# Turned copies of the input: laid out by the host and fetched, in place of two transposes and an eviction in each tile

## Chip, core and metric

The kernel runs on one NeuronCore of a Trainium2 chip. Its engines are TensorE (PE: matrix products; PEld is its weight load), VectorE (DVE), ScalarE (ACT), GpSimd (POOL) and SyncE (SP), which here only issues transfers. Each runs its own list of instructions in order and waits on semaphores for the others. The metric is the time of one execution on the device in microseconds, median of the runs.

## The reference

The input x is 8 x 750 x 256 in fp32. The calculation is one layer of three parts, each added to its input:

```python
# token mixing: segments of 256 tokens, every second token kept (128 rows per segment)
scores = einsum('bsqd,bskd->bsqk', x, x) / sqrt(256)
h = softmax(scores) @ x
# holographic attention, on layernorm(h)
bound = circ_conv(n, bind_key)                  # n = layernorm(h)
hologram = decay_matrix @ bound                 # causal, d ** (t - s)
h = h + n + gate * circ_corr(hologram, unbind_key)
# mixture of experts, on xf = layernorm(h), v = 0, two iterations:
#   shared control and 8 experts, of which 2 are chosen by a router, 512 -> 64 -> 768, gelu
#   integrator: sigmoid, softplus and a halting gate update (x, v)
# refining: 256 -> 512 -> 256 with gelu, times integration_weight
h = h + xf + integration_weight * refined
```

For a score product x . x^T of a 128-row tile TensorE needs x with its 256 features along the partitions, in two pieces of 128: the turned tile, xT.

## The kernel before

There are 24 tiles of 128 rows (8 batches of 3 segments; the third has 119 rows and is filled with zeros). The work is a software pipeline written out by hand: the function `slot(t)` of each engine is run for t = -3 to 26, and in one slot seven tiles are at work. z = t+3 is turned and its scores are computed; e = t+2 goes through exp; f = t+1 through attention, both layernorms, the scan, the router; t through the first expert iteration; n = t-1 through the second; m = t-2 through the integrator's end; o = t-3 through refining and output. What follows in which order on an engine is just the order of the code; waits are written by `passed(engine, semaphore, tile)`. A slot here is counted from TensorE's refining layer, ctl<-x2T (slot 3 is the first that has one).

For tile z in a slot, before the change: SP fetched the plain tile into one of six buffers xa (L299). TensorE turned it with two transposes into the PSUM bank pc (L623), after the scan of tile f had read that bank. ScalarE evicted it to the single buffer xT (L897, 128x256), between exp of tile e (L891) and the softplus of tiles m and t, for which another table of functions is loaded (L776). TensorE, after the 32 pieces of the experts' hidden layer (L427, pa<-x1T), multiplied xT with itself (L644) into pd, and VectorE scaled the scores and took their minimum (L1166, two records). Then xf of tile f was turned into pc (L652), which waited until xT had left that bank, and evicted by ScalarE (L793), after the table of the gelus (L787). Of xfT TensorE makes the router's hidden layer (L427, cd<-xfT; waits for xfT and for the scaled scores, which share the bank pd).

Ahead of the slots SP fetches the weights, all in one queue: the first plain tile, ident, the parameters `keeping(1)` (465 KB, from which ScalarE and VectorE make their constants), and so on. In the first slot that has a tile f (t = -1) ScalarE casts weights (`constants()`, L754 to L760), after the eviction of tile 2, and VectorE makes their low parts (`low_parts()`, L1023 and L1027), after xf of tile 0 and before the scaling of tile 2's scores. GpSimd computes u = xf - mu (L390) and base (L355, L357) from the same xf.

## Time and profile before

| | |
|---|---|
| median of 3 runs | 816.12 us (815.87 to 817.86) |
| the profiled execution | 814.5 us, of which the span from first to last instruction is 812.6 |
| TensorE products | 749.5 us busy, 92% of the span |
| TensorE weight loads | 650.0 us, 80% |
| VectorE | 651.9 us, 80% |
| ScalarE | 536.0 us, 66% |
| GpSimd | 274.1 us, 34% |
| chain that ended last | PE 46%, DVE 24%, ACT 21%, issue 8%, DMA 1% |
| mean granted TensorE clock | 0.966 of full speed |
| transfers | 14.13 MB in all; the 16 engines are 8 tenths busy in the first 20 us, 1 tenth in the next, near 0 after |

A profile is one execution. Engines overlap, so busy shares say which are full, not what bounds; the chain of waits says which piece of work, on which engine, every later piece was waiting for. A timeline row is start, duration, engine, line, operation, output and inputs, shapes; in brackets the idle time before it and what ended it. The granted clock is 1.00 at 2.4 GHz and 0.50 at 1.2 GHz.

### The profile page before, as it was taken

What the parts mean: (1) busy time and instruction counts of PE and PEld (TensorE: products, weight loads), DVE (VectorE), ACT (ScalarE), POOL (GpSimd) and SP (SyncE); (2) the same over time, 40 slices, a digit from 0 to 9 for tenths busy, and PEclk for the clock granted to TensorE, in tenths of its full rate; (3) what the DMA queues carried; (4) which work ended last, traced back from release to release, by engine and by line L of the source; (5) the groups of instructions that cost most, each with busy time, mean ns of one, the idle gap of its engine ahead of it and who ended that gap; (6) DMA issues with size and microseconds to landing.
All of it is one profiled execution on the core that took longest, in us unless ns stands there. A gap on an engine that the chain in (4) does not pass through costs nothing.

```text
span 812.6 us, 14659 instructions
## 1 busy us (share of the span) xinstructions
PE 749.5 (92%) x4784; PEld 650.0 (80%) x4784; DVE 651.9 (80%) x1516; ACT 536.0 (66%) x1334; POOL 274.1 (34%) x393
## 2 busy tenths in 40 slices
PE   4578999999999999999999999999999999999884
PEld 3466888888888888888888888888888888888764
DVE  3447778888889889889889889889889889889652
ACT  1555667677676676676676676685685785775554
POOL 1134333243253252243243243234234334333121
PEclk9577999999999999999999999999999999999997
DMA  8100000000000000000000000000000000000000
GB/s 336 52 8 1 1 1 14 1 15 14 1 14 11 5 14 7 8 15 1 15 13 2 14 14 1 14 14 1 14 14 2 8 8 1 8 8 1 7 8 13
DMA packets 8154, 14.13 MB, mean 17 GB/s; under 512 B 848, under 2 KB 7048, under 8 KB 7568
## 3 DMA queue, kind: packets, MB, share of 16 engines
q1 hardware_dynamic: 8080, 13.20, 4.6%
q8 instruction: 39, 0.64, 0.3%
q14 instruction: 35, 0.29, 0.1%
HBM read 10.05 MB, written 3.15 MB: 16 GB/s over the span
## 4 chain that ended last, share of the span: by engine, by line
PE 46%; DVE 24%; ACT 21%; issue 8%; DMA 1%; POOL 0%; ACTq 0%; POOLq 0%; SPq 0%; DVEq 0%
PE ctl L450 9%; PE ctl L466 7%; PE ctl L427 5%; ACT L776 3%; DVE hm_hi L1040 3%; PE pb L427 3%; ACT ge L809 3%; ACT L787 3%; PE ctl L469 2%; PE pa L427 2%; ACT work L779 2%; DVE both L1208 2%; ACT work L783 2%; PE cd L615 2%; DVE gl L1054 2%
## 5 line engine op out<-in xcount | busy, mean ns | idle before, releaser
L347 POOL TENSOR_TENSOR hm_lo<-gl,mexp 128x256 fp32r<-128x256 f32 x144 | 111.2, 797 | 358.5 <-DVE gl L1054 358.5
L450 PE MATMUL ctl<-w2e_hi,hm_hi 128*128 128x512 f32 (+1 forms) x432 | 160.6, 381 | 10.3 <-DVE hm_hi L1040 10.1
L450 PE MATMUL ctl<-w2e_lo,hm_hi 128*128 128x512 f32 (+1 forms) x432 | 149.6, 360 | 0.0
L827 ACT ACTIVATE work<-ctl 128x256 f32<-128x256 f32 (+1 forms) x144 | 70.6, 490 | 90.3 <-PE ctl L469 90.3
L450 PEld LDWEIGHTS ctl<-w2e_hi,hm_hi 128*128 128x128 f32 x432 | 82.1, 190 | 28.0 <-DVE hm_hi L1040 16.4
L466 PE MATMUL ctl<-w2e_hi,hm_lo 128*128 128x512 f32 (+1 forms) x432 | 102.3, 362 | 0.1
L1040 DVE TENSOR_TENSOR hm_hi<-ge,mexp 128x256 fp32r<-128x256 f32 x144 | 79.4, 579 | 22.3 <-ACT ge L809 16.1
L450 PEld LDWEIGHTS ctl<-w2e_lo,hm_hi 128*128 128x128 f32 x432 | 82.5, 191 | 11.1
L427 PE MATMUL pa<-x1T,par 128*128 128x128 f32 x768 | 89.7, 275 | 0.0
L427 PEld LDWEIGHTS pa<-x1T,par 128*128 128x128 f32 x768 | 87.8, 192 | 0.1
L466 PEld LDWEIGHTS ctl<-w2e_hi,hm_lo 128*128 128x128 f32 x432 | 74.3, 188 | 14.7 <-POOL hm_lo L347 0.8
L809 ACT ACTIVATE ge<-pa,par 128x128 f32<-128x128 f32 x192 | 54.6, 371 | 13.1 <-PE pa L427 13.1
L427 PE MATMUL pa<-xfT,par 128*128 128x128 f32 x384 | 55.8, 291 | 0.0
L829 ACT ACTIVATE work<-ctl 128x256 f32<-128x256 f32 x144 | 55.0, 382 | 0.0
L427 PEld LDWEIGHTS ctl<-x2T,par 128*128 128x128 f32 x384 | 47.9, 197 | 4.3 <-issue 1.3
L427 PEld LDWEIGHTS pa<-xfT,par 128*128 128x128 f32 x384 | 50.1, 203 | 1.1
L427 PE MATMUL ctl<-x2T,par 128*128 128x128 f32 x384 | 48.7, 282 | 1.5 <-issue 1.0
L456 PE MATMUL ctl<-w2a,hm_hi 128*128 128x512 f32 (+1 forms) x144 | 47.8, 386 | 0.0
L800 ACT ACTIVATE sh<-pb,par 128x128 f32<-128x128 f32 x48 | 17.6, 367 | 44.4 <-PE pb L427 44.4
L1070 DVE TENSOR_SCALAR work<-work,w 128x256 f32<-128x256 f32 x72 | 43.3, 655 | 2.9 <-ACT work L829 2.8
L469 PE MATMUL ctl<-w2b,end 128*128 128x512 f32 (+2 forms) x144 | 43.8, 358 | 1.3 <-ACT end L822 1.3
L949 ACT ACTIVATE end<-cd 116x256 fp32r<-116x256 f32 x24 | 9.2, 384 | 52.6 <-PE cd L721 52.6
(167 smaller groups left out, 1733.7 us busy)
## 6 DMA issues: line engine op xcount, KB each, us to landing
work<-params_dram SPq DMA_DIRECT2D x3, 1152.0 KB, 10.3
out_dram<-y SPq DMA_DIRECT2D x24, 128.0 KB, 1.7
xa<-x_dram SPq DMA_DIRECT2D x16, 128.0 KB, 2.7
par<-params_dram SPq DMA_DIRECT2D x1, 1280.0 KB, 12.8
work<-params_dram SPq DMA_DIRECT2D x2, 512.0 KB, 11.1
xa<-x_dram SPq DMA_DIRECT2D x8, 119.0 KB
par<-params_dram SPq DMA_DIRECT2D x1, 512.0 KB, 15.9
par<-params_dram SPq DMA_DIRECT2D x1, 465.0 KB, 4.6
```

The source lines that it names most:

```text
L347: TT(hm[1][:, j, c, :], gl[:, c, :], pairs(tile, j, c), ALU.mult).then_inc(done, 1)
L427: last = mm(dst[0:rows, c * P:(c + 1) * P], w[:, q, c, :], rhs[:, q, :], start=(q == 0), stop=(q == nk - 1))
L450: mm(dst[:, a:z], hm[0][:, j, c, :], w2e[i][:, c, a:z], start=(c == 0 and i == 0), stop=False)
L456: mm(dst[:, a:z], hm[0][:, j, PC, :], w2a[:, 1 + j, a:z], start=False, stop=False)
L466: mm(dst[:, a:z], hm[1][:, j, c, :], w2e[0][:, c, a:z], start=False, stop=False)
L469: last = mm(dst[:, a:z], end[tile.s][0:rows, j, :], w2b[0:rows, 1 + j, a:z], start=False, stop=True)
L776: nc.scalar.preload_act_table_set("softplus")
L809: last = AF(ge[:, c, :], pa[:, c * P:(c + 1) * P], ACT.Gelu, bias=par[:, a:a + 1])
L827: AF(tan[tile.s][:, 1:kinds, j, :], ctl_t[:, D:kinds * D].rearrange("p (a d) -> p a d", a=kinds - 1), ACT.Tanh, scale=0.5)
L829: AF(rb[tile.s][:, j, :], ctl_t[:, 0:D], ACT.Copy).then_inc(done, 1)
L1040: V.tensor_tensor(hm[0][:, j, c, :], ge[:, c, :], pairs(tile, j, c), ALU.mult).then_inc(done, 1)
L1070: last = V.tensor_scalar(gw[:, j, :], tan[m.s][:, 1, j, :], 1.0, w3[m.s][:, j:j + 1], ALU.add, ALU.mult)
```

## The change

The host lays the input out a second time: for each tile the kept rows, turned, 128 partitions x 256 (`_turned`). SP fetches that into three buffers xT, one for each segment of a batch; the first three are issued among the first transfers, the others each right behind the plain tile. The transposes, the eviction and their two semaphores are gone. The score product waits for the transfer, the attention product (L559) for the plain tile's transfer, which the transposes had waited for, and the transposes of xf for the scan of their tile, as the removed ones did.

```diff
@@ -103,7 +103,7 @@
 ENDS = [slice(0, HID), slice(HID, P)]
 
 
-def audio_layer(nc, x, params, out):
+def audio_layer(nc, x, turned_x, params, out):
     fp32, f32r, bf16 = mybir.dt.float32, mybir.dt.float32r, mybir.dt.bfloat16
     u32 = mybir.dt.uint32
     ALU, ACT, AX = mybir.AluOpType, mybir.ActivationFunctionType, mybir.AxisListType
@@ -172,7 +172,7 @@
 
 
         xa = [sb(f"xa{s}", [P, D]) for s in range(NX)]
-        xT = sb("xT", [P, KD, P])
+        xT = [sb(f"xT{s}", [P, KD, P]) for s in range(NS)]
         sc = sb("sc", [P, P])
         nmx = sb("nmx", [P, NS])
         ex = sb("ex", [P, P])
@@ -244,20 +244,21 @@
...
         x_in = [sem(f"x_in{s}") for s in range(NX)]
+        xT_in = [sem(f"xT_in{s}") for s in range(NS)]
...
@@ -298,14 +299,21 @@
                 src = x_pairs[bass.ds(tile.b * (SEQ // DIL) + tile.s * P, rows), 0:D]
                 sp.dma_start(xa[tile.x][0:rows, :], src).then_inc(x_in[tile.x], 16)
 
+            def turned_in(tile):
+                sp.dma_start(xT[tile.s][:, :, :].rearrange("p k m -> p (k m)"),
+                             turned_x[bass.ds(tile.n * P, P), :]).then_inc(xT_in[tile.s], 16)
+
             x_pairs = x.rearrange("(r two) d -> r (two d)", two=DIL)
+            turned_in(Tile(0, 0))
+            keeping(0)
             tile_in(Tile(0, 0))
-            keeping(0)
+            turned_in(Tile(0, 1))
             keeping(1)
             tile_in(Tile(0, 1))
             staging(0)
             sp.wait_ge(pad_zero, 1)
             tile_in(Tile(0, 2))
+            turned_in(Tile(0, 2))
             staging(1, E)
             staging(2)
             staging(5)
@@ -319,6 +327,8 @@
                 if z.exists() and z.low > 2:
                     passed(sp, att_ps, z, back=NX)
                     tile_in(z)
+                    passed(sp, score_ps, z, back=NS)
+                    turned_in(z)
                 if o.exists():
                     passed(sp, y_v, o)
                     sp.dma_start(out[bass.ds(o.n * P, P), :], y[o.s][:, :]).then_inc(y_out[o.s], 16)
@@ -536,8 +546,6 @@
                     passed(pe, ex_sb, f)
                     if t.exists():
                         passed(pe, me_sb, t, per=2, step=1)
-                    else:
-                        passed(pe, xT_sb, f)
                     nc.tensor.transpose(pc[:, 0:P], ex[:, :], ident).then_inc(eT_ps, 1)
                     if f.low == 0:
                         bound_and_back()
@@ -556,6 +564,7 @@
                         passed(pe, me_sb, t, per=2)
                     else:
                         passed(pe, smax_v, f.at(1))
+                    pe.wait_ge(x_in[f.x], 16 * (f.turn + 1))
                     mm(pd[:, 0:D], eT[:, :], xa[f.x][:, :], start=True, stop=True).then_inc(att_ps, 1)
 
                 if n.exists():
@@ -615,14 +624,6 @@
                         last = mm(pd[:, 0:D], holo[f.s][:, q, :], mix[:, q, :], start=(q == 0), stop=(q == KD - 1))
                     last.then_inc(retr_ps, 1)
 
-                if z.exists():
-                    pe.wait_ge(x_in[z.x], 16 * (z.turn + 1))
-                    if f.exists():
-                        passed(pe, scan_v, f)
-                    for q in range(KD):
-                        last = nc.tensor.transpose(pc[:, q * P:(q + 1) * P], xa[z.x][:, q * P:(q + 1) * P], ident)
-                    last.then_inc(xT_ps, 1)
-
                 if n.exists():
                     if t.exists():
                         passed(pe, e1_sb, t, per=2)
@@ -635,19 +636,18 @@
                     refine_lo(o)
 
                 if z.exists():
-                    passed(pe, xT_sb, z)
+                    pe.wait_ge(xT_in[z.s], 16 * (z.b + 1))
                     if f.exists():
                         passed(pe, mv2_v, f)
                     else:
                         passed(pe, smax_v, z, back=1)
                     for q in range(KD):
-                        last = mm(pd[:, 0:P], xT[:, q, :], xT[:, q, :], start=(q == 0), stop=(q == KD - 1))
+                        last = mm(pd[:, 0:P], xT[z.s][:, q, :], xT[z.s][:, q, :], start=(q == 0), stop=(q == KD - 1))
                     last.then_inc(score_ps, 1)
 
                 if f.exists():
                     passed(pe, xf_v, f)
-                    if z.exists():
-                        passed(pe, xT_sb, z)
+                    passed(pe, scan_v, f)
                     for q in range(KD):
                         last = nc.tensor.transpose(pc[:, q * P:(q + 1) * P], xf[f.s][:, q * P:(q + 1) * P], ident)
                     last.then_inc(xfT_ps, 1)
@@ -890,11 +890,6 @@
                     passed(act, eT_ps, e, back=1)
                     AF(ex[:, :], sc[:, :], ACT.Exp, scale=-1.0, bias=nmx[:, e.s:e.s + 1],
                        accum_out=esum[:, e.s:e.s + 1]).then_inc(ex_sb, 1)
-
-                if z.exists():
-                    passed(act, xT_ps, z)
-                    passed(act, score_ps, z, back=1)
-                    AF(xT[:, :, :].rearrange("p k m -> p (k m)"), pc[:, 0:D], ACT.Copy).then_inc(xT_sb, 1)
 
                 if t.exists():
                     softplus_of(m, t)
@@ -1293,6 +1288,15 @@
     return np.concatenate([a[n] for n, _ in _ALL], axis=1)
 
 
+def _turned(x):
+
+    import numpy as np
+    rows = np.zeros((BATCH, NS * P, D), np.float32)
+    rows[:, 0:SEQ // DIL] = x[:, ::DIL]
+    tiles = rows.reshape(NT, P, KD, P).transpose(0, 3, 2, 1)
+    return np.ascontiguousarray(tiles).reshape(NT * P, KD * P)
+
+
 def kernel(**inputs):
     import numpy as _np
     import concourse.bacc as _bacc
@@ -1300,7 +1304,8 @@
     from concourse.bass_utils import run_bass_kernel_spmd as _run
 
     i = {k: _np.asarray(v) for k, v in inputs.items()}
-    arrays = {"x_dram": _np.ascontiguousarray(i["x"].reshape(BATCH * SEQ, D)), "params_dram": _pack(i)}
+    arrays = {"x_dram": _np.ascontiguousarray(i["x"].reshape(BATCH * SEQ, D)), "turned_dram": _turned(i["x"]),
+              "params_dram": _pack(i)}
     nc = _bacc.Bacc("TRN2", target_bir_lowering=False, num_devices=1)
     args = [nc.dram_tensor(n, a.shape, _mybir.dt.from_np(a.dtype), kind="ExternalInput").ap()
             for n, a in arrays.items()]
```

On ScalarE, in a slot of the steady part, before:

```order
L891 ACTIVATE ex,esum<-sc,nmx 128x128
L897 ACTIVATE xT<-cd 128x256
L776 ACT_TABLE_LOAD
L779 ACTIVATE work<-work 128x768
L783 ACTIVATE work<-work 128x3x256
L787 ACT_TABLE_LOAD
L793 ACTIVATE xfT<-cd 128x256
```

and changed (exp, table, two softplus, table, eviction of xf):

```order
L891 ACTIVATE ex,esum<-sc,nmx 128x128
L776 ACT_TABLE_LOAD
L779 ACTIVATE work<-work 128x768
L783 ACTIVATE work<-work 128x3x256
L787 ACT_TABLE_LOAD
L793 ACTIVATE xfT<-cd 128x256
```

One row is gone, and nothing else moved. On ScalarE at the start, before (small holds constants, w2b and w2e_hi are casts of weights):

```order
L749 ACTIVATE small<-par 128x1
L750 ACTIVATE small<-par 128x1
L897 ACTIVATE xT<-cd 128x256
L891 ACTIVATE ex,esum<-sc,nmx 128x128
L897 ACTIVATE xT<-cd 128x256
L847 ACTIVATE eT<-cd 128x128
L891 ACTIVATE ex,esum<-sc,nmx 128x128
L897 ACTIVATE xT<-cd 128x256
L787 ACT_TABLE_LOAD
L754 ACTIVATE identb<-par 128x128
L756 ACTIVATE expandb<-work 8x512
L758 ACTIVATE w2b<-work 128x2304
```

and changed:

```order
L749 ACTIVATE small<-par 128x1
L750 ACTIVATE small<-par 128x1
L891 ACTIVATE ex,esum<-sc,nmx 128x128
L847 ACTIVATE eT<-cd 128x128
L891 ACTIVATE ex,esum<-sc,nmx 128x128
L787 ACT_TABLE_LOAD
L754 ACTIVATE identb<-par 128x128
L756 ACTIVATE expandb<-work 8x512
L758 ACTIVATE w2b<-work 128x2304
```

The table load and the casts now follow exp of tile 1 directly. On SP's queue, the first transfers before:

```order
L299 DMA xa<-x_dram 128x256
L288 DMA par<-params_dram 128x128
L288 DMA par<-params_dram 128x930
L299 DMA xa<-x_dram 128x256
L288 DMA work<-params_dram 128x1024
```

and changed:

```order
L303 DMA xT<-turned_dram 128x256
L289 DMA par<-params_dram 128x128
L300 DMA xa<-x_dram 128x256
L303 DMA xT<-turned_dram 128x256
L289 DMA par<-params_dram 128x930
L300 DMA xa<-x_dram 128x256
L289 DMA work<-params_dram 128x1024
```

The parameters for the constants (128x930) stand behind two more transfers.

## Rows read from the trace of the kernel before

**Rows 1.** Busy time by stretches of the trace; columns in the first line.
```profile
core 0: us, PE busy (x) PEld busy (x) DVE busy (x) ACT busy (x) POOL busy (x), PEclk, DMA share, GB/s
60.00:91.00 31.00, 26.95 (x150) 22.25 (x148) 21.58 (x49) 18.79 (x47) 13.10 (x17) 0.81 0.00 1
...
312.30:343.20 30.90, 30.17 (x201) 26.44 (x201) 26.92 (x63) 21.64 (x57) 11.13 (x16) 1.00 0.03 9
...
682.90:713.20 30.30, 29.43 (x194) 25.71 (x193) 26.45 (x60) 21.15 (x55) 11.78 (x16) 1.00 0.02 6
```

**Rows 2.** The chain of waits: start, length, what. Starts of slots 3, 21, 22.
```profile
127.07 1.79 PE ctl L427 x16
...
682.87 1.79 PE ctl L427 x16
...
713.25 1.79 PE ctl L427 x16
```

**Rows 3.** The chain of waits inside slot 8.
```profile
293.20 0.01 ACT xT L897
...
293.59 1.28 ACT L776
...
309.11 0.44 PE cd L736 x2
```

**Rows 4.** Timeline of ScalarE: slot 9 (two rows) and slot 21.
```profile
323.79 0.19 ACT L891 ACTIVATION_READ_ACCUMULATOR ex<-sc,nmx 128x1 f32 x1
...
324.50 1.28 ACT L776 ACT_TABLE_LOAD   x1
...
694.56 1.28 ACT L776 ACT_TABLE_LOAD   x1
```

**Rows 5.** Timeline of VectorE and GpSimd: slot 8, then slot 21.
```profile
295.76 1.38 DVE L1080 TENSOR_TENSOR work<-work 128x768 f32<-128x768 f32 x1 [0.24 <-ACT work L779]
297.18 0.69 DVE L1081 TENSOR_TENSOR both<-work 128x512 f32<-128x512 f32 x1
...
298.12 0.08 DVE L1166 DVE_READ_ACCUMULATOR sc<-cd 128x1 f32 x1
...
696.91 0.95 DVE L1080 TENSOR_TENSOR work<-work 128x768 f32<-128x768 f32 x1
697.89 1.10 DVE L1081 TENSOR_TENSOR both<-work 128x512 f32<-128x512 f32 x1
...
697.07 1.38 POOL L390 TENSOR_TENSOR u<-xf,par 128x256 f32<-128x256 f32 x1 [0.53 <-DVE xf L1153]
```

**Rows 6.** Timeline of TensorE: slot 8.
```profile
298.35 0.62 PE L427 MATMUL cd<-xfT,par 128*64 128x128 f32 x4
299.28 0.50 PE L450 MATMUL ctl<-w2e_hi,hm_hi 128*128 128x512 f32 x1 [0.31 <-DVE hm_hi L1040]
```

**Rows 7.** Timeline of the first 40 us: SP's queue, TensorE, ScalarE, VectorE, GpSimd.
```profile
2.11 0.43 SPq L299 DMA_DIRECT2D xa<-x_dram  x1
...
10.51 1.22 PE L644 MATMUL cd<-xT 128*128 128x128 f32 x4 [1.97 <-ACT xT L897]
...
21.84 0.38 ACT L897 ACTIVATE xT<-cd 128x256 f32<-128x256 f32 x1 [9.20 <-PE cd L623]
...
26.41 2.88 DVE L1023 SCALAR_TENSOR_TENSOR w2b<-w2b,par,work 128x768 fp32r<-128x768 f32 x3 [2.54 <-ACT w2b L758]
...
25.43 0.72 POOL L357 TENSOR_TENSOR base<-base,ib 128x256 f32<-128x256 f32 x1
...
32.07 1.08 PE L427 MATMUL cd<-xfT,par 128*64 128x128 f32 x4 [7.46 <-issue]
```

**Rows 8.** The chain of waits at the start and in slot 1.
```profile
1.65 4.61 DMA par<-params_dram
...
9.36 0.31 DVE sc L1166 x2
...
79.98 0.27 ACT xT L897
```

More of the change, by code:

```diff
@@ L250, in audio_layer @@
         dve_link = sem("dve_link")
-        (xT_ps, score_ps, eT_ps, att_ps, xnT_ps, retr_ps, xfT_ps, rh_ps, lg_ps, mT_ps, me_ps, s1_ps, e1_ps,
+        (score_ps, eT_ps, att_ps, xnT_ps, retr_ps, xfT_ps, rh_ps, lg_ps, mT_ps, me_ps, s1_ps, e1_ps,
          halt1_ps, u1_ps, x1T_ps, s2_ps, e2_ps, halt2_ps, u2_ps, x2T_ps, rl1_ps, rl2_ps) = (
-            sem(n) for n in ("xT_ps score_ps eT_ps att_ps xnT_ps retr_ps xfT_ps rh_ps lg_ps mT_ps me_ps s1_ps "
+            sem(n) for n in ("score_ps eT_ps att_ps xnT_ps retr_ps xfT_ps rh_ps lg_ps mT_ps me_ps s1_ps "
                              "e1_ps halt1_ps u1_ps x1T_ps s2_ps e2_ps halt2_ps u2_ps x2T_ps rl1_ps rl2_ps").split())
-        (xT_sb, ex_sb, eT_sb, xfT_sb, rh_sb, tw_sb, mT_sb, me_sb, s1_sb, e1_sb, th1_sb, u1_sb, x1T_sb, s2_sb,
+        (ex_sb, eT_sb, xfT_sb, rh_sb, tw_sb, mT_sb, me_sb, s1_sb, e1_sb, th1_sb, u1_sb, x1T_sb, s2_sb,
          e2_sb, th2_sb, u2_sb, x2T_sb, rg_sb, sp1_sb, sp2_sb, gh1_sb, gh2_sb,
          rgh_sb, eb1_sb, eb2_sb) = (
-            sem(n) for n in ("xT_sb ex_sb eT_sb xfT_sb rh_sb tw_sb mT_sb me_sb s1_sb e1_sb th1_sb u1_sb x1T_sb "
+            sem(n) for n in ("ex_sb eT_sb xfT_sb rh_sb tw_sb mT_sb me_sb s1_sb e1_sb th1_sb u1_sb x1T_sb "
                              "s2_sb e2_sb th2_sb u2_sb x2T_sb rg_sb sp1_sb sp2_sb gh1_sb gh2_sb rgh_sb eb1_sb eb2_sb").split())
```

## Prediction

> **What bounds the kernel now.** I read the busy time by stretches first [rows 1]. In a slot of the steady part TensorE is busy 30.17 of 30.90 us; so a stage is worth anything only where it can be heard through a nearly full TensorE. Then the whole chain of waits, for the length of a slot: the 16 pieces of the refining layer begin at 127.07 in slot 3 and at 682.87 in slot 21, 18 slots, 30.88 us each [rows 2]. Then the chain inside one slot [rows 3]. It has three legs: TensorE from the transposes of x2 (309.11) through the next slot's products up to the hidden layer of the shared expert; then ScalarE for about 9.5 us (two gelus, a table load, exp, **the eviction into xT**, a table load, two softplus, a table load, the eviction into xfT, four gelus, the split copy); then VectorE up to x2. TensorE stands still in the last two legs only for moments: 0.31 us before the expert product, which waits for the masked units [rows 6]. So ScalarE's leg decides, and the eviction that goes is a link of it: the table load of L776 starts at 293.59, where exp's read-out was over and the eviction could begin at 293.20.
>
> **What goes, per slot.** (a) The eviction on ScalarE. In one slot of three, as that of rows 3, 293.59 - 293.20 = 0.39 us. In the two others it also waited for its transposes: read-out of exp ends at 323.79 + 0.19 = 323.98, table load at 324.50 [rows 4]; without it the load follows after 0.02, so 0.50. Over 18 slots 12 x 0.50 + 6 x 0.39 = 8.3. (b) Two transposes on TensorE, 0.22 us from start to start; they lie ahead of a stall, so they are no gain of their own, but TensorE has to come earlier too if ScalarE's 0.50 is to be passed on: 0.22 and the 0.31 of the stall cover it. (c) Transposes of xf no longer wait for the eviction; they came long after it: nothing.
>
> **The slot that is already without it.** Slot 21 has no tile to prepare: no transposes, no eviction, no score product, no scaling of scores. From 682.87 to 713.25 it takes 30.38 us [rows 2], 0.50 less than the mean, with TensorE at 29.43 of 30.30 busy and the granted clock at 1.00 [rows 1]; its table load starts at 694.56 [rows 4], 0.20 after exp's read-out began. 18 x 0.50 = 9.0. It also lacks the score product and VectorE's scaling, which stay in the changed kernel, so it is the upper end; I take 8.5 for the 18 slots.
>
> **What is late next in a slot.** The first product of the router waits for xfT and for VectorE's scaling of the scores. The scaling's read-out ends at 298.12 + 0.08 = 298.20 and that product starts at 298.35 [rows 5, 6]: they stand 0.15 apart, so the scaling must come earlier as well. Ahead of it VectorE does L1080 and L1081. Before, L1080 waited 0.24 us for a softplus, started at 295.76 and took 1.38, because GpSimd was in its own operation on xf; in slot 21, where the softplus came earlier, it started at 696.91, ahead of GpSimd (697.07, which then took 1.38 in place of 0.73), and took 0.95, and L1081 took 1.10 in place of 0.69 [rows 5]. From the moment at which VectorE was free for L1080 to the end of L1081 that is 297.18 + 0.69 - (295.76 - 0.24) = 2.35 before and 697.89 + 1.10 - 696.91 = 2.08 in slot 21. So the scaling comes about 0.3 earlier, and so does the router's product; 0.1 to 0.2 that it lacks to ScalarE's 0.50 is slack, since ScalarE gets to that product's gelu only after the four gelus of the experts.
>
> **The first slots.** In slot 1 the piece of the eviction that shows in the chain is 0.27 [rows 8]; slot 2 has the same piece, slot 0 I estimate at 0.4 like a steady one. Together 0.9.
>
> **The start** is where the change is largest and least sure. ScalarE stood 9.20 us until the third tile's transposes, evicted at 21.84, and only then loaded its table and cast the weights; VectorE waited 2.54 us for the first cast, until 26.41, with xf ready at 23.87 [rows 7]. From 26.41 to the router's first product at 32.07 the work is a fixed string of 5.66 us. Changed, ScalarE goes on to the casts from 21.84 - 9.20 = 12.64 on, as the weights land, and has 11 us for a table load and two casts; VectorE then starts when xf is there: 2.54 gained at most. Against it, three things. First, two more transfers are issued ahead of the parameters that feed ScalarE's and VectorE's constants; an issue takes 0.43 [rows 7], so those land 0.86 late at least, and if the 256 KB also move ahead of the 465 KB that took 4.61 from issue to landing [rows 8], up to 256/465 x 4.61 = 2.5 more. I take 1.2, near the lower end, since the two transfers move while the later ones are issued. Second, in favour: the score product of tile 1 stood at 10.51 for its eviction [rows 7], though the scaling of tile 0 was over at 9.36 + 0.31 = 9.67 [rows 8]; this gives 0.8 back. Net delay of the string 0.4. Third, VectorE now meets GpSimd: three operations of GpSimd on xf and h2, of 0.72 each, the last at 25.43 [rows 7], were finished before VectorE began at 26.41; now they fall on it. One such meeting cost VectorE 0.41 (1.10 against 0.69, rows 5), three make 1.2. Start: 2.54 - 0.4 - 1.2 = 0.9, bounded by 2.54 (no delay) and by 2.54 - 2.6 - 2.2, a loss of 2.3.
>
> That the one waits for the other is what rows 5 show on both sides; how much of the other it waits for is open between 0.41 and the whole 0.72 (rival 3). The Trainium skill (SBUF — State Buffer, section "SBUF: two separate sides") says that a VectorE operation with two inputs in SBUF and a GpSimd operation that reads SBUF take a shared port pair in turns, whichever comes second waiting for the whole of the other. By that the sum is the one of rival 3, by rows 5 the one below; slot 21's VectorE waited for less than the rule has it.
>
> **Nothing for the transfers in the slots.** A turned tile is issued right behind its plain tile, a slot and more ahead of its use, and the transfer engines are at 0.03 of their time there [rows 1]. SP's new wait (score of the tile three before) is for a product two slots old, so the output behind it in the queue is not held. TensorE's new wait for the plain tile in the attention product is for a transfer of slots ago.
>
> **Sum.** 8.5 + 0.9 + 0.9 = 10.3. The profiled execution of before took 814.5 us (span 812.6 and 1.9 around it), so 804.2; the median of the runs, 816.12, lies 1.6 above that execution, and I forecast the median: 805.8 us.
>
> **Rivals.**
> 1. VectorE's scaling doesn't move (GpSimd gets ahead of L1080 as before). The router's product stays at 298.35, its gelu can come only 0.2 earlier, and a slot gains 0.2 to 0.25 although ScalarE is free sooner: 18 x 0.22 = 4.0, with the 0.9 of the start and the 0.9 of the first slots 5.8 gained, 810.3. Against it: slot 21 did it the other way. 0.10.
> 2. TensorE's clock in the first slots. From 60 to 91 the granted clock is 0.81 on average [rows 1], that is 38% of 31 us at 1.2 GHz, after a stretch in which TensorE stood still for parts of slot 0. With 0.4 us less standing still there the clock may stay at 2.4 GHz: up to 0.19 x 31 = 5.9 less, 799.9. For it: nothing else stands ahead of that stretch. Against it: most of the standing still remains. 0.07.
> 3. At the start VectorE waits for the whole of each GpSimd operation: 3 x 0.72 = 2.2 in place of 1.2; the start gives 2.54 - 0.4 - 2.2 = 0, the sum is 9.4, the time 806.7. It differs from the forecast by less than the runs do, but its trace is another one: the string of 5.66 us takes 7.9. 0.15.
> 4. The gain is swallowed within measuring (another engine's string just as late everywhere), 815 to 817: slot 21 speaks against it. 0.02.
> 5. Slower: TensorE's clock falls in the steady part, because it now has less work in a slot. Price: a slot of 30.17 us of TensorE at half speed, some 25 to 30 us more, so 830; a microsecond at 1.2 GHz costs half of one, so it decides once more than 2 x 10.3 = 21 us of the steady part are run so. Slot 21, with still less work than a changed slot will have, kept 1.00. 0.03, with whatever else could make it slower by as much.
>
> **How the numbers follow.** The forecast has 0.63. Its own width: the start from a loss of 2.3 to a gain of 2.5, the slots from 7.3 (18 x 0.39 and a little more) to 9.0, 0.5 us of run to run; 803.5 to 809. The range takes in part of rival 2 and stops short of rival 1's centre: 802.8 to 809.6. A change under 0.3% (2.4 us) can't be told from none here; rivals 4 and 5 alone lie there or beyond: faster 0.95, same 0.02, slower 0.03.
>
> **What would show it.** Right: slots of 30.4 us throughout, all three kinds alike; L776 0.02 behind exp's read-out; L1080 near 0.95 us and GpSimd's operation on xf stretched to 1.4; the casts on ScalarE before 24, VectorE's low parts right behind xf but with three GpSimd operations between them, the string at 6.9 us in place of 5.66; the router's first product near 31.2. Wrong: L1080 still at 1.38 and slots near 30.65 (rival 1); a stretch of the granted clock that differs between 44 and 91; the parameters landing later than 7.5 us; or a new wait ahead of the score product.

## The result, and the profile after

| | before | changed |
|---|---|---|
| median of the runs | 816.00 us | 806.23 us |
| lowest, highest, runs | 813.73, 817.86, 4 | 804.91, 806.45, 4 |
| profiled execution, its span | 814.5, 812.6 us | 804.9, 803.1 us |
| granted clock, whole span | 0.966 | 0.968 |

The ratio is 0.9878, with a 95% interval from 0.9851 to 0.9905: 9.8 us faster. The forecast was 805.8 us (802.8 to 809.6). The transfers grow from 14.13 to 17.28 MB; the host's work of laying the input out a second time is not in the metric.

In the changed kernel the lines of its own file moved: L427 is now L437 (hidden and refining products), L450 is L460 (experts), L592 is L601, L615 is L624, L644 is L645, L541 is L549, and on VectorE L1080 is L1075, L1081 is L1076, L1166 is L1161, L1114 is L1109, L1128 is L1123, L1023 is L1018; on GpSimd L390 is L400. ScalarE's lines up to L891 kept their numbers.

**The length of a slot.** The chain of waits of the changed kernel: start, length, what. Slots 3, 4, then 8, 9, 10, then 21 and 22.
```profile
125.25 1.79 PE ctl L437 x16
155.68 1.79 PE ctl L437 x16
...
277.43 1.78 PE ctl L437 x16
307.87 1.79 PE ctl L437 x16
338.33 1.79 PE ctl L437 x16
...
673.24 1.79 PE ctl L437 x16
703.67 1.79 PE ctl L437 x16
```
From 125.25 to 673.24 are 18 slots: 30.44 us each, where [rows 2] gave 30.88. That is 18 x 0.44, or 682.87 - 127.07 - (673.24 - 125.25) = 7.81 us. The kinds are nearly alike now: 30.43 for slot 3, 30.44 for slot 8, 30.46 for slot 9. Up to slot 3 the changed kernel leads by 127.07 - 125.25 = 1.82, and from slot 21 on it loses 0.13, since 803.1 - 673.24 is 129.86 and 812.6 - 682.87 is 129.73. Together 9.5, the difference of the two spans.

**ScalarE's leg in slot 8.** Timeline of ScalarE: start, length, engine, line, operation.
```profile
288.96 0.19 ACT L891 ACTIVATION_READ_ACCUMULATOR ex<-sc,nmx 128x1 f32 x1
289.17 1.28 ACT L776 ACT_TABLE_LOAD   x1
...
293.36 0.39 ACT L793 ACTIVATE xfT<-cd 128x256 f32<-128x256 f32 x1
```
The table load stands 0.02 behind the end of exp's read-out, 0.21 behind its start. In [rows 3] the eviction stood between them, in [rows 4] the eviction and its wait.

**VectorE, GpSimd and TensorE in slot 8**, from their timelines; in square brackets the idle time before, and what ended it.
```profile
291.39 0.95 DVE L1075 TENSOR_TENSOR work<-work 128x768 f32<-128x768 f32 x1
292.38 1.10 DVE L1076 TENSOR_TENSOR both<-work 128x512 f32<-128x512 f32 x1
...
293.73 0.08 DVE L1161 DVE_READ_ACCUMULATOR sc<-cd 128x1 f32 x1
```
```profile
291.56 1.38 POOL L400 TENSOR_TENSOR u<-xf,par 128x256 f32<-128x256 f32 x1 [0.53 <-DVE xf L1148]
```
```profile
293.96 0.62 PE L437 MATMUL cd<-xfT,par 128*64 128x128 f32 x4
294.87 0.49 PE L460 MATMUL ctl<-w2e_hi,hm_hi 128*128 128x512 f32 x1 [0.29 <-DVE hm_hi L1035]
```
This is slot 21 of [rows 5] to the hundredth: 0.95, 1.10, and 1.38 on GpSimd, with VectorE ahead. The expert product still stands for the masked units, 0.29 in place of the 0.31 of [rows 6].

**Stretches**, the same columns as in [rows 1]: us, busy time of TensorE, its weight loads, VectorE, ScalarE, GpSimd, then clock, transfers, GB/s.
```profile
60.00:91.00 31.00, 27.18 (x141) 22.17 (x142) 20.40 (x48) 18.16 (x44) 13.10 (x17) 0.81 0.02 5
307.90:338.30 30.40, 29.93 (x199) 26.21 (x199) 26.81 (x63) 21.24 (x56) 11.79 (x16) 1.00 0.05 14
```
TensorE is busy 29.93 of 30.40 us, and the granted clock stays 1.00: the two transposes are gone, and the slot shrank by more than they had filled.

**The start.** Timelines of ScalarE, VectorE, GpSimd and TensorE in the first 33 us.
```profile
7.39 0.20 ACT L749 ACTIVATE small<-par 128x1 f32<-128x1 f32 x1 [5.38 <-DMA par<-params_dram]
...
13.04 1.28 ACT L787 ACT_TABLE_LOAD   x1
...
17.09 2.11 ACT L760 ACTIVATE w2e_hi<-work 128x2304 fp32r<-128x2304 f32 x1
```
```profile
23.82 0.41 DVE L1148 TENSOR_SCALAR xf<-h,mv,rs 128x256 f32<-128x256 f32 x1 [0.94 <-POOL rs L396]
24.15 3.81 DVE L1018 SCALAR_TENSOR_TENSOR w2b<-w2b,par,work 128x768 fp32r<-128x768 f32 x3
27.88 3.07 DVE L1022 TENSOR_TENSOR w2e_lo<-work,w2e_hi 128x2304 fp32r<-128x2304 f32 x1
```
```profile
24.32 1.43 POOL L400 TENSOR_TENSOR u<-xf,par 128x256 f32<-128x256 f32 x1 [0.53 <-DVE xf L1148]
...
27.22 1.32 POOL L367 TENSOR_TENSOR base<-base,ib 128x256 f32<-128x256 f32 x1
```
```profile
31.26 1.09 PE L437 MATMUL cd<-xfT,par 128*64 128x128 f32 x4 [6.28 <-issue]
```
The casts stand from 13.04 on and are over at 19.20, far ahead of xf. VectorE no longer waits: it begins its low parts at 24.15, 2.26 earlier than the 26.41 of [rows 7]. But the three of them take 3.81 in place of 2.88, and GpSimd's three operations at the same time take 1.43, 1.43 and 1.32 in place of 0.72 each. From VectorE's start to the router's first product it is 31.26 - 24.15 = 7.11 us, where it was 5.66: of the 2.26 there remain 0.81.

### The profile page after: what moved, and what is told of

It reads as the page before. It is cut to its first block, busy times and chain, and to the rows that moved or that the text cites. A ratio compares the mean times of both kernels' runs of the same rounds, so it can differ in the third digit from the quotient of the medians.

```text
span 803.1 us, 14519 instructions
## 1 busy us (share of the span) xinstructions
PE 743.1 (93%) x4736; PEld 644.9 (80%) x4736; DVE 651.7 (81%) x1516; ACT 528.7 (66%) x1310; POOL 288.2 (36%) x393
## 2 busy tenths in 40 slices
DMA packets 11611, 17.28 MB, mean 22 GB/s; under 512 B 1232, under 2 KB 10504, under 8 KB 11024
## 4 chain that ended last, share of the span: by engine, by line
PE 42%; DVE 25%; ACT 24%; issue 8%; DMA 1%; POOL 0%; SPq 0%; POOLq 0%; ACTq 0%; DVEq 0%
PE ctl L460 9%; PE ctl L476 7%; PE ctl L437 5%; ACT L776 4%; ACT L888 4%; DVE hm_hi L1035 3%; ACT L787 3%; ACT ge L809 3%; PE pb L437 3%; PE ctl L479 2%; PE pa L437 2%; ACT work L779 2%; DVE both L1203 2%; ACT work L783 2%; DVE gl L1049 2%
## 5 line engine op out<-in xcount | busy, mean ns | idle before, releaser
L460 PE MATMUL ctl<-w2e_hi,hm_hi 128*128 128x512 f32 (+1 forms) x432 | 160.4, 381 | 8.6 <-DVE hm_hi L1035 8.2
L460 PE MATMUL ctl<-w2e_lo,hm_hi 128*128 128x512 f32 (+1 forms) x432 | 149.4, 360 | 0.0
L460 PEld LDWEIGHTS ctl<-w2e_hi,hm_hi 128*128 128x128 f32 x432 | 82.2, 190 | 26.2 <-DVE hm_hi L1035 14.6
L460 PEld LDWEIGHTS ctl<-w2e_lo,hm_hi 128*128 128x128 f32 x432 | 82.4, 191 | 11.1
L437 PEld LDWEIGHTS pa<-x1T,par 128*128 128x128 f32 x768 | 89.4, 192 | 1.1
L437 PE MATMUL pa<-x1T,par 128*128 128x128 f32 x768 | 89.6, 275 | 0.0
L437 PE MATMUL pa<-xfT,par 128*128 128x128 f32 x384 | 55.6, 291 | 0.0
L437 PEld LDWEIGHTS ctl<-x2T,par 128*128 128x128 f32 x384 | 47.8, 197 | 4.3 <-issue 1.3
L437 PEld LDWEIGHTS pa<-xfT,par 128*128 128x128 f32 x384 | 49.9, 202 | 1.1
L437 PE MATMUL ctl<-x2T,par 128*128 128x128 f32 x384 | 48.6, 281 | 1.5 <-issue 1.0
L381 POOL TENSOR_TENSOR rg_lo<-rg,rg_hi 128x512 fp32r<-128x512 f32 x24 | 31.1, 1297 | 35.5 <-ACT rg_hi L772 35.5
```

The source lines that it names most:

```text
L437: last = mm(dst[0:rows, c * P:(c + 1) * P], w[:, q, c, :], rhs[:, q, :], start=(q == 0), stop=(q == nk - 1))
L460: mm(dst[:, a:z], hm[0][:, j, c, :], w2e[i][:, c, a:z], start=(c == 0 and i == 0), stop=False)
```

## Experiments

Each is the changed kernel with an edit; those of e1, e2, e9 and e10 add work whose result nobody reads. Slot length is that of slots 3 to 20 from the chain of waits; the last column is the start of the router's first product.

| | median us | kernel before, same chip | ratio, 95% | slot us | router us |
|---|---|---|---|---|---|
| changed | 806.23 | 816.00 | 0.9878 (0.9851 to 0.9905) | 30.44 | 31.26 |
| e1 copy on ScalarE | 811.75 | 815.47 | 0.9966 (0.9948 to 0.9984) | 30.71 | 31.37 |
| e2 transposes back | 809.45 | 815.47 | 0.9924 (0.9896 to 0.9953) | 30.53 | 31.54 |
| e3 GpSimd first | 815.63 | 815.47 | 0.9995 (0.9979 to 1.0010) | 30.86 | 31.78 |
| e4 GpSimd late | 804.90 | 815.47 | 0.9881 (0.9856 to 0.9906) | 30.42 | 31.11 |
| e5 GpSimd off the start | 804.43 | 814.66 | 0.9870 (0.9839 to 0.9902) | 30.43 | 30.26 |
| e6 parameters first | 803.83 | 814.66 | 0.9864 (0.9835 to 0.9892) | 30.43 | 28.91 |
| e7 ScalarE held at the start | 805.85 | 814.66 | 0.9897 (0.9861 to 0.9933) | 30.43 | 32.94 |
| e8 = e4 + e5 + e6 | 802.45 | 814.66 | 0.9847 (0.9818 to 0.9875) | 30.43 | 27.94 |
| e9 slots as before, start as changed | 815.49 | 815.45 | 1.0002 (0.9987 to 1.0018) | 30.86 | 32.58 |
| e10 transposes and wait, no eviction | 807.81 | 815.45 | 0.9897 (0.9875 to 0.9920) | 30.52 | 31.27 |

**e1_copy.** A copy of a constant of the eviction's size, into a buffer that nobody reads, where the eviction stood.
```diff
+                if z.exists() and z.low > 2:
+                    AF(spare[:, :], pv("iw"), ACT.Copy)
                 if t.exists():
                     softplus_of(m, t)
```


> The changed kernel with one copy more on ScalarE (128x256, of a constant, into a buffer that nobody reads) where the eviction of xT stood, in the 21 slots from t = 0 on. Theory (ScalarE's leg sets the slot): the copy takes 0.36 to 0.38 us and all of it is heard, a slot goes from 30.44 to 30.8 us, 18 slots 6.7 us and the first three 1.1 more: 806.2 + 7.8 = 814.0 us. Rival (TensorE or VectorE set the slot of the changed kernel): 806 to 808.

The slot is 0.27 longer: (680.83 - 127.98) / 18 = 30.71. Timeline of ScalarE in this kernel, slot 8:
```profile
293.02 0.18 ACT L892 ACTIVATION_READ_ACCUMULATOR ex<-sc,nmx 128x1 f32 x1
293.12 0.40 ACT L896 ACTIVATE spare<-par 128x256 f32<-128x256 f32 x1
293.52 1.28 ACT L777 ACT_TABLE_LOAD   x1
```
The copy waits for nothing and so begins under the read-out, 0.10 behind its start; the table load stands 0.50 behind the read-out's start, against 0.21 without the copy, so ScalarE gave away 0.29, and the slot shows 0.27. ScalarE's leg is the one that decides, and what is laid on it is heard nearly whole; only the size of the piece was 0.3 and not 0.36.

VectorE in the same slot, its first product:
```profile
295.69 1.47 DVE L1078 TENSOR_TENSOR work<-work 128x768 f32<-128x768 f32 x1 [0.16 <-ACT work L780]
```
GpSimd had begun its operation on xf at 295.61, so it is ahead again, as in the kernel before; in slots 9 and 10 VectorE stays ahead (0.96). The slots take 30.73, 30.70 and 30.70 us all the same: while ScalarE is this late, the order costs nothing of its own.

**e2_turns.** The two transposes back on TensorE, with their waits; nobody reads what they make.
```diff
+                if z.exists():
+                    pe.wait_ge(x_in[z.x], 16 * (z.turn + 1))
+                    if f.exists():
+                        passed(pe, scan_v, f)
+                    for q in range(KD):
+                        nc.tensor.transpose(pc[:, q * P:(q + 1) * P], xa[z.x][:, q * P:(q + 1) * P], ident)
                 if n.exists():
...
                     hidden(pa, P, w1e, range(EC), x1T, 2 * KD, e2_ps)
```


> The changed kernel with the two transposes put back on TensorE at their old place in each of 24 tiles; nobody reads what they write. Theory (they lie ahead of a moment in which TensorE waits): the 0.22 us a slot go into the 0.29 us that the expert product waits; router's product 0.2 later, which leaves ScalarE's gelu 0.0 to 0.06 late; slot 30.44 to 30.5, time 806 to 807.5. Rival (TensorE's list is full): 0.22 x 21 = 4.6 more, 810.8.

30.53, so +0.09 and not nothing. It is not spread evenly; e10 below has where it goes.

**e3_u_first.** VectorE's products wait until GpSimd has made its operation on xf, so that the order of the kernel before is back, without the eviction.
```diff
                 if m.exists() and not last_in:
+                    if f.exists():
+                        passed(dve, u0_g, f)
                     products(m)
```


> The changed kernel in which VectorE's L1075 waits until GpSimd is through with u = xf - mu, so that GpSimd goes first and VectorE no longer overtakes it. This is rival 1 of the prediction made true. Theory: L1075 starts at about the end of u, 0.9 us later than now, both VectorE operations then run unhindered (0.95 and 0.69), the scaling ends 0.5 later than now, the router's product starts 0.5 later and ScalarE's gelu 0.3 later: slot near 30.75, 18 x 0.3 = 5.4 more, 811.6. Rival (slack there is larger than read): slot unchanged at 30.44, 806.2.

The whole gain is gone: 815.63 against 815.47, slots of (683.10 - 127.70) / 18 = 30.86. VectorE and TensorE in this kernel, slot 8:
```profile
296.92 0.96 DVE L1075 TENSOR_TENSOR work<-work 128x768 f32<-128x768 f32 x1 [0.84 <-POOL u L400]
```
```profile
299.08 0.62 PE L437 MATMUL cd<-xfT,par 128*64 128x128 f32 x4 [0.52 <-DVE sc L1163]
```
The router's product begins 299.08 - 282.04 = 17.04 us into its slot (the slot starts at 282.04), against 293.96 - 277.43 = 16.53 in the changed kernel: 0.51 later. ScalarE, at the gelu of what that product makes, now stands for it:
```profile
299.75 0.36 ACT L919 ACTIVATE rh<-cd,par 64x128 f32<-64x128 f32 x1 [0.23 <-PE cd L437]
```
The slot is 0.42 longer than the changed one on the mean, where I expected 0.3. So ScalarE's 0.4 can't be had in full unless VectorE's scaling of the scores comes earlier with it. How much is left without that, this run doesn't measure, since the edit puts the product later than the kernel before had it (17.04 against 298.35 - 281.52 = 16.83). An estimate: the gelu begins 17.71 into the slot here and began at 17.67 in the kernel before; with the product 0.21 earlier it would begin at 17.50, so about 0.2 a slot would be left, which is what rival 1 had.

**e4_u_late.** The reverse: GpSimd's operation on xf waits for the largest score, so it comes behind L1076.
```diff
                     passed(pool, x1_v, f, back=NS)
+                    if z.exists() and z.low > 2:
+                        passed(pool, smax_v, z)
                     TT(u0[f.s][:, :], xf[f.s][:, :], pv("mu"), ALU.subtract)
```


> The changed kernel in which GpSimd's u waits until VectorE has scaled the scores (tiles 3 to 23), so that L1076 isn't held up by it. Theory: L1076 takes 0.69 in place of 1.10 and the scaling comes 0.41 earlier, but the router's product is not what ScalarE waits for, so the slot stays 30.44 and the time 806.2. Rival (the scaling still sets when the router's product and with it the leg ends): slot 0.1 to 0.4 shorter, 799 to 804.

L1076 is back at 0.69 us and the scaling comes earlier, but VectorE then stands 0.98 before the masked units; slots 30.42. Once VectorE is ahead of GpSimd, more lead has no worth.

**e5_gpsimd_off_start.** GpSimd's first operation on xf waits until VectorE's low parts of the weights are done.
```diff
+                    if f.low == 0:
+                        pool.wait_ge(set_dve, 2)
                     TT(u0[f.s][:, :], xf[f.s][:, :], pv("mu"), ALU.subtract)
```


> The changed kernel in which GpSimd's three operations at the start (u and base of tile 0) wait until VectorE has made the low parts. Theory (VectorE pays for meeting GpSimd): the low parts go back from 3.81 + 3.07 us to 2.88 + 2.55, the router's first product from 31.26 to about 29.9, time 1.4 less, near 804.8, read with some 1 to 2 us of scatter from when TensorE's clock rises in the first 75 us. Rival (something else stretched them, as ScalarE's traffic or transfers): no change of either duration.

VectorE's timeline at the start of this kernel:
```profile
24.61 2.87 DVE L1020 SCALAR_TENSOR_TENSOR w2b<-w2b,par,work 128x768 fp32r<-128x768 f32 x3
27.39 2.55 DVE L1024 TENSOR_TENSOR w2e_lo<-work,w2e_hi 128x2304 fp32r<-128x2304 f32 x1
```
2.87 and 2.55 in place of 3.81 and 3.07, and the router's product 30.26 - 24.61 = 5.65 us behind VectorE's start, which is the string of before (5.66). So the 1.45 us by which the string had grown were the meetings with GpSimd. In the time of the kernel the 1.0 us is inside the scatter.

**e6_params_first.** The parameters are fetched ahead of the first two tiles and their turned forms.
```diff
+            keeping(1)
             turned_in(Tile(0, 0))
             keeping(0)
             tile_in(Tile(0, 0))
             turned_in(Tile(0, 1))
-            keeping(1)
```


> The changed kernel with the parameters for the constants (465 KB) first in SP's queue, ahead of the turned and plain tiles. Theory (the two transfers put ahead of them delayed the start by 1.1 us, from 6.28 to 7.39): ScalarE's first constant near 5.4, the router's first product 1.5 to 2 us earlier than 31.26 unless the weights for bind and unbind land later, time 804.2 to 804.8. Rival (the start is held by the big weights): the constants come earlier and the router's product stays within 0.3 of 31.26.

ScalarE's first constant, from its timeline in this kernel:
```profile
4.30 0.20 ACT L749 ACTIVATE small<-par 128x1 f32<-128x1 f32 x1 [2.29 <-DMA par<-params_dram]
```
4.30 in place of 7.39, and the router's first product at 28.91 in place of 31.26, 2.35 earlier, more than the 1.5 to 2 expected, as the constants too came earlier than the 5.4 expected. The time, 803.83, is below the changed kernel's, but the intervals of the two ratios overlap.

**e7_hold_scalar.** At the start ScalarE waits, before its table load and casts, as long as it did before the change, without the eviction.
```diff
+                if z.exists() and z.low == 2:
+                    passed(act, retr_ps, f)
                 if t.exists():
                     softplus_of(m, t)
```


> The changed kernel in which ScalarE waits, in the slot that casts weights, for the first retrieval product, as it waited for the third tile's transposes before the change; so the casts start at about 21.8 in place of 13.0. Theory: the first cast ends near 25.9, VectorE's low parts start there in place of 24.15, meet only the last GpSimd operation, and the router's first product is at 31.6 to 31.8 in place of 31.26: 0.4 later, 806.6. So of the start's gain the freed ScalarE is worth only 0.4, since GpSimd's meetings eat the rest. Rival (the early casts are worth the 2.5 us they are earlier): 808.7, router's product at 33.7.

VectorE waits again (1.70 for w2b) and starts at 26.90, when two of GpSimd's three operations are over; all three take 0.72 or 0.73, and only the last meets VectorE, whose product takes 3.26 there (2.87 without GpSimd in e5, 3.81 in the changed kernel). What that saves is less than the later start costs. From xf's start to the router's product it is 32.94 - 24.78 = 8.16, against 31.26 - 23.82 = 7.44: 0.72 lost, where I expected 0.4. In the time nothing of it can be seen (805.85).

**e9_slots_back.** Transposes, wait and eviction back, the eviction from t = 0 on and into a buffer that nobody reads; the transfers, and ScalarE's list at the start, stay as changed.
```diff
+                    if z.low > 2:
+                        passed(act, turn_ps, z)
+                        AF(spare[:, :], pc[:, 0:D], ACT.Copy).then_inc(turn_sb, 1)
                 if t.exists():
                     softplus_of(m, t)
...
                     passed(pe, scan_v, f)
+                    if z.exists() and z.low > 2:
+                        pe.wait_ge(turn_sb, (z.n + 1) - 3)
```


> The slots as before the change, the start as changed: the two transposes are back on TensorE, ScalarE evicts them (128x256) into a buffer that nobody reads, in the 21 slots from t = 0 on, and the transposes of xf wait for that eviction; the scores still use the fetched tile. Theory (the slots carry the gain): slots of 30.88 as before, 18 x 0.44 = 7.9 and three first slots 0.9 more than changed, 815.0. Rival (the start carries much of it): 812 or less.

815.49 against 815.45, slots 30.86: nothing is left of the gain. ScalarE in slot 8 of this kernel:
```profile
294.99 0.19 ACT L903 ACTIVATION_READ_ACCUMULATOR ex<-sc,nmx 128x1 f32 x1
295.17 0.38 ACT L909 ACTIVATE spare<-cd 128x256 f32<-128x256 f32 x1
295.57 1.28 ACT L788 ACT_TABLE_LOAD   x1
```
VectorE's first product takes 1.38 us again behind 0.25 of waiting, as in [rows 5]. This is what says where the gain is: in the slots, the first three included. A gain of 0.81 us at the start, if it reaches the end at all, lies within the 1.1 us by which this interval reaches below 1; the profiled execution has none of it, with its parameters late and the router's first product at 32.58.

**e10_wait_only.** The same transposes, and ScalarE waits for them, but evicts nothing: what is the wait worth without the work?
```diff
+                if z.exists() and z.low > 2:
+                    passed(act, turn_ps, z)
                 if t.exists():
                     softplus_of(m, t)
```


> As the run with the slots put back, but ScalarE only waits for the transposes and evicts nothing. Theory (of the 0.44 of a slot 0.3 is the eviction's own time and 0.15 came from its waiting for the transposes and the delay that these bring): slot 30.55 to 30.65, 808.5 to 810. Rival (the waiting is nothing, the whole is ScalarE's eviction): slot 30.53 as with transposes alone.

30.52, as e2 without the wait: the rival was right. The chain of waits of this kernel, slots 8 to 10:
```profile
279.72 1.79 PE ctl L438 x16
310.13 1.79 PE ctl L438 x16
340.70 1.79 PE ctl L438 x16
```
30.41 for slot 8 and 30.57 for slot 9. Over slots 3 to 20 one slot in three (the kind of slot 8) costs nothing more than in the changed kernel, the other two 0.12 each, and 0.14 in e2. Two kinds stand in the kernel before too, in its chain of waits, slots 8 to 10:
```profile
281.52 1.79 PE ctl L427 x16
312.30 1.79 PE ctl L427 x16
343.19 1.79 PE ctl L427 x16
```
30.78 and 30.89. What tells the kinds apart is in VectorE's timeline of the kernel before, slots 8 and 9:
```profile
291.01 0.73 DVE L1128 TENSOR_TENSOR_SCAN holo<-decays,cd 128x128 f32<-128x128 f32 x2
...
321.81 0.85 DVE L1128 TENSOR_TENSOR_SCAN holo<-decays,holo,cd 128x128 f32<-128x128 f32 x2
```
A tile that begins a sequence scans from nothing (0.73); the two that follow carry the state (0.85), in the changed kernel as well. The two transposes stand behind the scan on TensorE, and the transposes of xf behind them. Where the delay ends is in ScalarE's timeline of slot 9, first of the changed kernel, then of e2, in which nobody waits for the two transposes:
```profile
323.79 0.38 ACT L793 ACTIVATE xfT<-cd 128x256 f32<-128x256 f32 x1
```
```profile
326.52 0.38 ACT L800 ACTIVATE xfT<-cd 128x256 f32<-128x256 f32 x1 [0.16 <-PE cd L659]
```
In the changed kernel the eviction of xfT begins 323.79 - 307.87 = 15.92 us into the slot and waits for nothing. In e2 ScalarE stands 0.16 for the transposes of xf and begins 16.06 into it (the slot starts at 310.46): 0.14 later, and the slot is 0.13 longer (30.59 against 30.46). In slot 8 of e2, behind the shorter scan, it begins at 15.92 with no wait, and the slot takes 30.41. So the 0.22 of the two transposes fit ahead of ScalarE in the slots that begin a sequence, and not in the others.

**e8_all.** e4, e5 and e6 in one kernel.


> The changed kernel with three orders altered together: parameters first in SP's queue, GpSimd's operations of the start after the low parts, and u after the scaling of the scores in every slot. Theory: router's first product near 28 (31.26 - 1.4 - 1.8), slots 30.42 as with u late: 802.6 to 803.5. Rival (the clock's rise decides the first 75 us whatever the work does): as the changed kernel with u late, 804.9.

802.45 us, the fastest of all. Slots of 30.43, like the changed kernel's; slot 3 begins at 122.44 in place of 125.25, and the router's first product at 27.94. It beats the kernel before clearly (0.9818 to 0.9875). Over the changed kernel it is ahead by 0.3% in the ratios, and the intervals overlap, so this last step is likely and not shown.

## Why the forecast held, and where its terms were off

**What bounds a slot.** ScalarE's leg, as forecast. e1 lays 0.29 us on it and the slot grows by 0.27; e9 puts everything back and the slot is 30.86. The step that could have failed is that VectorE's scaling of the scores had to come earlier too; e3 shows that the full gain needs it, and its rows fit rival 1's 0.22 a slot for the case that it doesn't, as an estimate.

**The size in the slots: 7.8 in place of 8.5.** The pieces on ScalarE were right. In slot 8 the table load had begun 293.59 - 293.01 = 0.58 us behind the read-out's start and now begins 0.21 behind it: 0.37; in slot 9 it was 324.50 - 323.79 = 0.71 and is now 0.20: 0.51. ScalarE's timeline of the changed kernel, slot 9:
```profile
319.40 0.19 ACT L891 ACTIVATION_READ_ACCUMULATOR ex<-sc,nmx 128x1 f32 x1
319.60 1.28 ACT L776 ACT_TABLE_LOAD   x1
```
Forecast were 0.39 and 0.50, in 18 slots 8.3. Two things lie between the 8.5 and the 7.8. One is the 0.2 that the forecast added to the 8.3 on the strength of slot 21; they did not come. The other lies ahead of that leg: from the slot's start to exp's read-out it was 11.50 us and is 11.53, the mean of slots 3 to 20 (11.49 and 11.53 in slots 8 and 9). In 18 slots that is 0.5 us, which the forecast had at nothing. A part of it is to be seen on TensorE, at the weights for its transposes of xn in slot 8, first in the kernel before, then in the changed one:
```profile
289.30 0.20 PEld L592 LDWEIGHTS cd<-par,xn 128*128 128x128 f32 x2 [0.32 <-DVE xn L1114]
```
```profile
285.25 0.20 PEld L601 LDWEIGHTS cd<-par,xn 128*128 128x128 f32 x2 [0.37 <-DVE xn L1109]
```
They start 7.78 us into the slot before and 7.82 after (7.79 and 7.81 on the mean), and in VectorE's timeline xn itself starts at 6.41 (287.93) and 6.44 (283.87). TensorE stood for VectorE's xn before the change as well, 0.32 and now 0.37, so VectorE's string at the head of the slot was no hidden leg that the change laid bare; it was open in both. Slot 21, taken as the upper end, is longer too: 30.38 before, 703.67 - 673.24 = 30.43 now, in a slot in which nothing was removed. Why VectorE comes to this string 0.03 later, counted from TensorE's refining layer, is open.

**The transposes on TensorE** were to be worth nothing of their own. e2 and e10 make it 0.08 to 0.09 a slot: nothing in the slots that begin a sequence, 0.12 to 0.14 in the two others. The step that failed is the slack: the forecast laid the 0.22 against the 0.31 that TensorE stands before the expert product, but where it is felt first is ScalarE's eviction of xfT (e10). The rest of the 0.44, 0.35 (30.88 less 30.53), is the eviction; e9 less e10 gives 0.34 to 0.35 in every kind of slot. That is more than e1's 0.27, since a copy that waits for nothing starts under exp's read-out, and the eviction did not. For the order of VectorE and GpSimd e1 finds no price of its own while ScalarE is as late as that. The forecast had read the difference of 0.11 between its two kinds of slot as a wait for the transposes. It is one, but what makes them late is the scan.

**The start: 0.81 in place of 0.9**, out of three terms that each stood near their measure, in one execution of each kernel. The delay of the constants was put at 1.2 and is 7.39 less 6.28, 1.11 (before, ScalarE's first constant stood at 6.28, right behind the transfer of [rows 8]). The net delay of the string was put at 0.4: xf comes at 23.82, where it was ready at 23.87 in [rows 7] and so had started at 23.45, 0.37 later. Three meetings with GpSimd were put at 1.2 and are 1.45, or 0.49 each; rival 3, the whole of each GpSimd operation (2.2), is out. e5 shows that they are these meetings. The first two terms are in part luck: in the eight other kernels with the same first transfers (all but e6 and e8) ScalarE's first constant stands between 6.68 (e10) and 7.98 (e9), so the delay could have been measured at 0.4 or at 1.7; and in the kernels whose work in the first 30 us is the changed kernel's but for transposes that nobody reads (e1 to e4, e9, e10) the router's first product stands between 31.11 and 32.58. The third comes again: w2b takes 3.80 or 3.81 and w2e_lo 3.07 in all of these six.

**The first slots** were to give 0.9. Up to slot 3 the lead is 1.82, the forecast's 1.8 for both. I don't count this as a hit: by the router's first product of each slot the lead goes from 0.81 to 2.75 in slot 0, 1.57 in slot 1 and 1.81 in slot 2, and in this part the clock changes between its levels, at other times in the two kernels. Here one sign of being wrong did come, a stretch of the clock that differs: from 44 to 91 it is 0.81 before and 0.78 now, from 38 to 60 it is 0.73 before and 0.81 now, over both (38 to 91) 0.78 and 0.81. An estimate from the last pair: 0.03 of 53 us, up to 1.6 us, could be the clock's and not the change's. From slot 21 on, 0.13 were lost that no term had. Rival 2 asked for 5.9 us and didn't come, since the stretch from 60 to 91 has a clock of 0.81 in both kernels. But what it said of the place was right: that is where a kernel of this family can win or lose microseconds by chance. Rival 5, a clock that falls in the steady part, is out: 1.00 from 75 to 760 us.

**The rest of what was to be seen** came so: L1075 at 0.95, the read-out's neighbour at 0.02, the casts before 24 (over at 19.20), the string at 7.11 (forecast 6.9), the router's first product at 31.26 (31.2), the parameters at 7.39 (not later than 7.5).

## What to carry to other kernels

Look in the trace of before for a stretch in which the operation to be removed is already missing (here slot 21): it shows which engine is late next and in which order two engines then meet (here to the hundredth), and it bounds the gain (9.0 for the 18 slots, of which 7.8 came). When a leg is shortened, or work is put on another engine, ask of every wait along the leg by how many hundredths it is met; here the scaling of the scores had to move along for the full gain (e3), and the transposes of xf come so close ahead of ScalarE that 0.22 on TensorE costs 0.14 in two slots of three and nothing in the third (e2). And work that is started earlier may meet another engine's: of 2.3 us won by an earlier start 1.45 went to that.

## What was not expected of the hardware

**VectorE and GpSimd at the same time.** When they meet, both are longer, also where they share no tensor: in a slot VectorE works on work, GpSimd on xf and par. GpSimd's operation of 0.72 took 1.43, 1.43 and 1.32 at the start and 1.38 in a slot; VectorE lost 1.45 us to the three at the start (e5 takes it away again) and 0.41 to the one in the slot (1.10 against the 0.69 that L1076 takes in e3 and e4). The Trainium skill (SBUF — State Buffer, section "SBUF: two separate sides") has it that the one that starts first keeps the ports that both use for its whole instruction, and that the other is blocked until then. The trace agrees that the second waits, in either order, but not quite in the size: where VectorE came second it lost 0.43 in slot 8 of the kernel before (1.38 against 0.95) with 0.56 of GpSimd's operation still to run, 0.39 in e7 with 0.58 to run, and 0.52 in slot 8 of e1 (1.47) with 0.65 to run. It lost 0.13 to 0.19 less than the rest each time; why, no run here shows.

**The clock in the first 75 us differs from kernel to kernel and from run to run.** Its two levels are 1.2 and 2.4 GHz. Windows of 2 us of the changed kernel:
```profile
36.00:38.00 2.00, 1.77 (x10) 1.77 (x10) 0.69 (x6) 0.91 (x3) 0.00 (x0) 0.52 0.00 0
38.00:40.00 2.00, 1.60 (x11) 0.91 (x9) 0.01 (x1) 1.68 (x6) 0.00 (x0) 1.00 0.00 0
...
50.00:52.00 2.00, 1.01 (x6) 0.58 (x6) 0.62 (x3) 1.97 (x3) 1.40 (x4) 0.89 0.18 41
72.00:74.00 2.00, 2.00 (x10) 1.62 (x9) 0.32 (x1) 0.14 (x1) 0.74 (x1) 0.99 0.00 0
```
And of the kernel before:
```profile
44.00:46.00 2.00, 2.00 (x9) 1.62 (x9) 1.22 (x5) 0.00 (x0) 1.29 (x2) 0.90 0.04 7
54.00:56.00 2.00, 0.53 (x3) 0.53 (x4) 0.00 (x0) 1.41 (x2) 2.00 (x2) 0.66 0.00 0
```
The clock was granted in full from about 38 to 51.5 in the one and from about 44.5 to 54.5 in the other, each time after the router's first product at 31 to 32, then at half until about 72, and in full again from there. In the experiments the first rise lay at 38 (e4), 40.5 (e8), 43 (e5, e6), 46 (e1, e2, e3, e10) and 47 to 47.5 (e7, e9). The changed kernel and e10 have the router's first product 0.01 us apart (31.26 and 31.27) and the first rise 8 us apart. What decides it is not shown. Runs of the kernel before went from 811.4 us, with a mean clock of 0.975 over the span, to 819.0, with 0.962. So half a dozen of microseconds go with the clock by chance, and a gain of one microsecond at the start, like the 0.81 above, is seen in the trace and not in the time.

**A copy begins under a read-out.** With nothing to wait for, ScalarE's copy in e1 began 0.10 us behind the start of exp's read-out of 0.18; the eviction of e9, which waits for its transposes (over at 295.13), began 0.18 behind it. A piece of 0.40 us was therefore worth 0.29.
